# Summing attention weights of a graph layer: one product after an add on VectorE, in place of five accumulating products

## The reference

```
h = h @ W                                   # 1024 x 1024
al, ar = h @ a[0, :d], h @ a[0, d:]
e = exp(-leaky_relu(al[src] + ar[dst], 0.1))
rowsum  = segment_sum(e, src)               # one number per node
h_prime = segment_sum(e[:, None] * h[dst], src)
out = x + elu(h_prime / (rowsum[:, None] + 1e-5))
```

## Time and profile before

| | |
|---|---|
| median of 3 executions | 2250.3 us |
| profiled execution, its own time | 2243.76 us |
| its span, first to last instruction | 2242.3 us |
| busy in the span: TensorE, weight loads | 1697.4 us, 925.2 us |
| VectorE, ScalarE, GpSimd | 1131.4 us, 401.0 us, 1366.9 us |
| mean granted TensorE clock | 0.823 of full |
| `collect` (layer 1), from its first to its last instruction | about 1510 us to 2242 us |

### The profile page before, as it was taken

One profiled execution on the slowest core, in us unless ns is written; L12 is line 12 of the kernel. 1 busy time (PEld: TensorE's weight loads), 2 busy tenths in 40 slices (PEclk: granted clock), 3 DMA queues, 4 the chain that ended last, 5 costly groups with the idle time before them and its releaser, 6 DMA issues. The chain is left out here.

```text
span 2242.3 us, 27665 instructions
## 1 busy us (share of the span) xinstructions
PE 1697.4 (76%) x10226; PEld 925.2 (41%) x10226; DVE 1131.4 (50%) x2763; ACT 401.0 (18%) x791; POOL 1366.9 (61%) x1296
## 2 busy tenths in 40 slices
PE   3685937668812878888777987845899999999997
PEld 2332413224301544545444544521355544445454
DVE  5564824548611566677676676652333333333331
ACT  1111201111100121222211222211222222122221
POOL 1566675567776566666676666207676666676740
PEclk9787967879965777777778777766998999999898
DMA  7221402203208999999999999629999999999971
GB/s 226 67 58 41 116 23 61 69 27 111 70 19 333 329 347 341 348 359 366 355 363 346 352 352 369 199 78 405 380 352 352 361 351 355 353 373 349 365 247 43
DMA packets 186965, 561.17 MB, mean 250 GB/s; under 512 B 45714, under 2 KB 50167, under 8 KB 186469
## 3 DMA queue, kind: packets, MB, share of 16 engines
q0 software_dynamic: 139776, 416.40, 51.8%
q1 hardware_dynamic: 43448, 129.78, 17.0%
q10 hardware_dynamic: 3600, 13.16, 1.6%
HBM read 554.33 MB, written 53.28 MB: 271 GB/s over the span
## 5 line engine op out<-in xcount | busy, mean ns | idle before, releaser
L940 POOL DMA_INDIRECT ring<-layer_rows,idx x360 | 412.5, 1146 | 230.8 <-PE acc L1065 114.4
L412 POOL DMA_INDIRECT src_lists<-pay_T,slot_T x392 | 407.8, 1040 | 214.9 <-issue 129.9
L1503 POOL DMA_INDIRECT ring<-layer_rows,idx x360 | 366.6, 1018 | 184.7 <-issue 91.8
L508 PE MATMUL mm<-w_sb,hT 128*128 128x512 f32 x800 | 381.5, 627 | 26.9 <-issue 26.8
L1065 PE MATMUL acc<-ring,weight 128*32 128x256 f32 (+1 forms) x3600 | 329.0, 485 | 6.7 <-DVE weight L1172 3.7
L508 PEld LDWEIGHTS mm<-w_sb,hT 128*128 128x128 f32 x800 | 157.6, 202 | 215.5 <-issue 215.5
L1565 PE MATMUL acc<-ring,weight 128*32 128x512 f32 x1600 | 213.2, 628 | 36.6 <-ACT weight L1513 19.1
L1065 PEld LDWEIGHTS acc<-ring,weight 128*32 128x32 f32 (+1 forms) x3600 | 149.7, 137 | 125.9 <-issue 83.6
L1665 DVE TENSOR_TENSOR hT_low<-tp_l,hT_high 128x512 fp32r<-128x512 f32 x50 | 34.6, 691 | 316.5 <-issue 223.5
L1016 PE MATMUL turned<-ident,edge_a 128*16 128x128 f32 (+1 forms) x125 | 38.8, 311 | 193.9 <-ACT edge_a L952 93.7
L1598 PE MATMUL mm_l<-w_high,hT_high 128*128 128x512 f32 x400 | 169.3, 423 | 4.6 <-issue 2.6
(11 more groups left out here) (232 smaller groups left out, 2184.4 us busy)
## 6 DMA issues: line engine op xcount, KB each, us to landing
layer_rows<-row_l ACTq DMA_DIRECT2D x25, 514.0 KB
layer_rows<-row_l SPq DMA_DIRECT2D x25, 514.0 KB
own<-layer_rows SPq DMA_DIRECT2D x25, 512.0 KB
x<-xb SPq DMA_DIRECT2D x25, 512.0 KB
x1t<-x SPq DMA_DIRECT2D x25, 512.0 KB
xt<-in_x_dram SPq DMA_DIRECT2D x24, 512.0 KB
xb<-in_x_dram SPq DMA_DIRECT2D x24, 512.0 KB
out_dram<-y SPq DMA_DIRECT2D x24, 512.0 KB
```

What stands on the lines that cost most here:

```text
L412: pool.indirect_dma_start(out=list_d, out_offset=bass.IndirectOffsetOnAxis(ap=slot_T[:, b:b + 1], axis=0), in_=pay_T[:, b:b + 1], in_offse ...
L508: last = pe.matmul(mm[k][:, f * HALF:(f + 1) * HALF], hT[k][:, c, :], w_sb[:, c, f * HALF:(f + 1) * HALF], start=c == 0, stop=c == KC - 1)
L940: pool.indirect_dma_start(out=ring[:, t % 2, blocks(c), :][:, q, :], out_offset=None, in_=table0, in_offset=bass.IndirectOffsetOnAxis(ap=i ...
L1503: pool.indirect_dma_start(out=fetched(t, c)[:, q, :], out_offset=None, in_=table1, in_offset=bass.IndirectOffsetOnAxis(ap=idx, axis=0), bo ...
```

## The change

`add_weights` on TensorE had five accumulating products per tile, each of a 128x128 block of weights (one round) with a column of ones. Now VectorE adds the five blocks elementwise into a new tile `weight_sum` (one reduce over 128x640 elements, with the rounds as the innermost axis), and TensorE multiplies that with the ones once. TensorE waits for `weights_added`; VectorE waits for the last Exp of the tile and, before it overwrites `weight_sum`, for the previous product. On VectorE the new step stands at the end of step (u, 3), behind `split(u-1, 1)`.

```
@@ semaphores and tiles
+        weight_sum = sb("weight_sum", [P, P])
+        weights_added = sem("weights_added")
@@ TensorE
             def add_weights(t):
                 if t >= 1:
                     pe.wait_ge(inv_done, t)
-                for c in range(RC):
-                    last = pe.matmul(sums[:, 0:1], weight[t % 2][:, c, :], ones[:, :], start=c == 0, stop=c == RC - 1)
-                last.then_inc(total_done, 1)
+                pe.wait_ge(weights_added, t + 1)
+                pe.matmul(sums[:, 0:1], weight_sum[:, :], ones[:, :], start=True, stop=True).then_inc(total_done, 1)
@@ VectorE
+            def add_weights(t):
+                dve.wait_ge(weighed, RC * t + RC)
+                if t >= 1:
+                    dve.wait_ge(total_done, t)
+                dve.tensor_reduce(weight_sum[:, :], weight[t % 2][:, :, :].rearrange("p c n -> p n c"), AX_X, ALU.add)\
+                    .then_inc(weights_added, 1)
@@ VectorE, the list of steps
                 if c == 3 and 1 <= u <= TILES:
                     split(u - 1, 1)
+                if c == 3 and u < TILES:
+                    add_weights(u)
```

## The result

| | before | after |
|---|---|---|
| median | 2247.6 us (4 runs, 2233.7 to 2278.0) | 2362.4 us (4 runs, 2351.4 to 2381.3) |
| ratio | 1 | 1.054, 95% interval 1.044 to 1.064 |
| span of the profiled execution | 2242.3 us | 2349.3 us |
| layer 1, from the first gather issued to the end | 731.0 us (from 1511.3) | 852.6 us (from 1496.7) |
| mean tile | 27.0 us | (2278.37 - 1632.19) / 20 = 32.3 us |

What follows compares the result with a forecast made beforehand. The prediction took TensorE's own program to bound layer 1. The profiled 2243.8 us plus 94 us of net delay plus 44 us of low clock gave 2382 us, own range 2345 to 2425 (0.63), wider range 2322 to 2440.

Steps and rivals of the forecast that it cites:

- TensorE's chain bounds layer 1: Layer 1: gathered data lie ready and TensorE's program is late; floor 23.4 us a tile, mean 27.0 us.
- The saving, 0.91 us a tile, 23 us: TensorE's `add_weights`: four of five products go, 0.91 us a tile at full clock, 23 us or 1.0% in all.
- When the sum is ready: `weight_sum` ready at 2181.3 us, TensorE there at 2176.1: a 5.2 us wait, 4.3 us net of the saving.
- The reduce, 0.82 us: VectorE's new reduce behind `split(u-1, 1)`: 0.82 us, from the 128x512 reduce and a 640-element operation; 1.1 us by the strided row.
- The price that the prediction made of it, 1.5 us: VectorE's strided reduce at double cost per element: about 1.5 us, total 16 us higher at 2398 us, chance 0.08.
- The clock, 2.3 us in a tile: TensorE falls to the low clock behind each new wait: 2.3 us in each of 19 tiles, 44 us.
- Rival A: TensorE's clock holds through the new waits: 2338 us, chance 0.18.
- B: TensorE's low-clock stretches are long, 12.4 us each: 2456 us, chance 0.11.
- The short waits of the kernel before: TensorE's waits of 1.45 us in some tiles; their possible absence was counted as nothing and left to the low side.
- 94 + 44 = 138: Layer 1's added time: 94 us of net delay from TensorE's waits over the tiles, 44 us from the low clock.
- C: Gathers set the tile and TensorE's new wait fills time it would have waited anyway: 2260 us, chance 0.05.
- D: VectorE has the sum before TensorE needs it, so 23 us are gained: 2221 us, chance 0.03.

Runs made afterwards that it cites:

- e2_wait_only: Kernel before, five products and no reduce, with TensorE waiting in front of them for `split(u-1, 1)`: 2260.0 us, ratio 1.079.
- e1_early: Changed kernel with the reduce moved on VectorE to step (u, 2), ahead of `split(u-1, 0)`: 2090.7 us, ratio 0.998.
- e4_strides: Kernel before plus three unread 128x640 reduces on VectorE, with 4, 16 and 512 bytes between added elements: 2096.2 us, one run.
- e10_middle: Changed kernel with the reduce on VectorE in step (u, 3) ahead of `weigh(5u+5)`: 2138.3 us, ratio 1.020.
- e6_behind_multiply: Changed kernel with TensorE's one product moved behind `multiply(u-1, (0, 1, 2))`: 2102.1 us, ratio 1.005.

## Why the prediction was right

The sign and the mechanism (TensorE waits for a reduce that is late in VectorE's order, and the wait lowers its clock) are shown. That the time came so close, 2362 us against 2382, is in part luck, as the third and the sixth point below say. By its steps:

- **TensorE's chain bounds layer 1.** Held: a wait put into it (e2_wait_only) costs its full length. What the prediction lacked is how near the next limit is. It read GpSimd's waits for ring places as proof of room; on the chips without the short waits the room is 0.1 us a tile.
- **The saving, 0.91 us a tile, 23 us.** The product shrank as said. As a gain it is hardly to be had on those chips: e1_early realizes 3 us, GpSimd's pace takes the rest.
- **When the sum is ready.** The order of steps was right. The wait was sized at 5.2 us and is 7.27 in most tiles: 0.4 us by the reduce, 1.4 us by ScalarE before `keep_high(u-1, 1)`, 0.5 us by a later first `keep_high` (2172.37 - 2171.20 = 1.17 us behind the start of `turn`, against 0.69 us), less 0.2 us that TensorE already waits before its second transpose. On the other chip, where the reduce is most of what is off, it is 5.75 us. Tile 1, which the sum counted, has no wait; the last one pays 4.2 us and not 1.5.
- **The reduce, 0.82 us.** Mis-sized: 1.22 us. The error was in setting aside the one strided row, whose bound was 1.1. The Trainium skill, SBUF — State Buffer, section "Door 1: The DMA port swizzle", says that each access that crosses to a new 16-byte line pays a penalty. The traces agree: 1.28 and 1.34 us where every read is in a new line, 0.81 where it is not [e4_strides]. The price that the prediction made of it, 1.5 us, is somewhat high, and 16 bytes cost as much as 512.
- **The clock, 2.3 us in a tile.** Right: 2.3 on the first chip, 2.5 on the other. In each of the 22 tiles with a full wait, on either chip, the records of `multiply` behind it are at 0.63 us. Rival A, that the clock holds, falls; so does B, since the low stretch ends within `multiply`. The Trainium skill, TensorE: Matmul & The Clock Gate, section "HAM oscillation — how this bites in real kernels", tells of a kernel that restarts at the low clock in every tile behind a wait, and these traces agree.
- **The short waits of the kernel before.** Counted as unchanged, but for a credit in the four tiles with a long wait; in fact they are gone from the tile (0.20 us before the second transpose where some had 4.1), 3.6 us a tile. For a full tile the forecast was 4.3 + 2.3 = 6.6 us; with the idle time longer by 2.3 (7.5 against 5.2) and these 3.6 taken off it is 5.3, which is measured. So two errors of size met: the wait was too short, and the kernel before was given too little back. That they nearly cancel is luck: by my estimate from these numbers the first alone would have given 2382 + 23 x 2.3 = 2435 us, and the second alone about 2313 us, under the stated range. Layer 1 got 122 us longer where 94 + 44 = 138 were forecast. Why the short waits vanish is not shown.
- **Rivals.** The prediction's C (the gathers set the tile) and D (VectorE is first) fall with the change as it is: TensorE waits for VectorE in the tile, and GpSimd waits for TensorE. C's mechanism, with GpSimd in the place of the DMA engines, governs the repaired version.

The best of the tried versions that leave nothing out, e1_early, has the ratio 0.998 (0.997 to 0.999) to the kernel before: a difference clear of 1, and too small to matter.

## What to carry to other kernels

Work taken off a busy engine and given to an idle one is paid by where it stands in the idle engine's program: look up what the new instruction is queued behind and what is queued behind the one that waits for it, before counting the cycles saved. On these chips the same reduce cost 7.6%, 2.0% or nothing by three places in one list. Before reckoning with a gain of 1 us in a loop, divide the other engines' fixed pace by the same loop; here 18 issues of 1.296 us left 0.1 us of it.

## What was not expected of the hardware

- A reduce over elements 16 or 512 bytes apart takes 1.34 and 1.28 us, over neighbours 0.81 us (128x640, float32).
- Waits of TensorE of 2.28 us brought the clock down in about every second tile (e10_middle), those of 1.25 us in none (e6_behind_multiply). The two also differ in what stands around the wait, so the length alone is not shown to decide.
- Chips differ in how they run the same kernel: 2093 or 2248 us. On one kind, waits of 1.3 to 1.5 us on ScalarE and GpSimd, for which the profile names no releaser, stand in most tiles while gathers run; on the other I found none. What they wait for is open, and so is whether they account for the whole difference between the chips.
